# FFN norms of six images: the channel sums split into a high and a low part before TensorE adds them up

## The chip, the core and the metric

The kernel runs on one core of one Trainium2 chip. The metric is the device time of one execution in microseconds (us). A core has five engines that run their own instruction lists side by side: TensorE (PE in the profile, its weight loads PEld), VectorE (DVE), ScalarE (ACT), GpSimd (POOL) and SyncE (SP), which here only issues DMAs. They meet only at semaphores: an instruction waits until a counter has reached a value. SBUF is the on-chip memory of 128 partitions, PSUM the eight banks that TensorE writes.

## The reference, cut to what matters

Two layers run over 8 images of 384 channels and 32x32 pixels. Layer 0 is a Mamba mixer and an FFN, layer 1 a displaced 5x5 convolution and an FFN. Only the norm ahead of each FFN is touched here. Each pixel is normed over its 384 channels:

```python
def _ln_t(v, eps=1e-5):
    m = jnp.mean(v, axis=-1, keepdims=True)
    s = jnp.var(v, axis=-1, keepdims=True)
    return (v - m) / jnp.sqrt(s + eps)

def _bitlinear(x, W, b):
    Wb = _binarize_weights_groupwise(W)          # signs of W around the mean of each of 5 groups
    y = jnp.einsum('btc,oc->bto', x, Wb) + b
    return _quantize_activations_groupwise(y)    # scaled by the largest |y| of a group of images

h = _bitlinear(x, W1, b1)                        # 384 -> 1536
h = jax.nn.gelu(h, approximate=False)
out = _bitlinear(h, W2, b2)                      # 1536 -> 384

t = t + _L0_ffn_ref(_ln_t(t), ...)               # once in each layer
```

With 5 groups over 8 images a group is one image, and the last three images come out of the FFN as zeros. So each layer has five FFN images, ten in all.

## The kernel before, in words

An image lies in SBUF as `xn`, three tiles of 128 channels (partitions) by 1024 pixels. Everything of a norm is done in two halves of 512 pixels (`HALVES`, `half(h)`).

The norm of FFN image f goes through four engines:

- GpSimd adds the three tiles of `xn` into `xsum` (`sum_tiles`, L2193 and L2195), elementwise, 128x1024 each.
- TensorE multiplies `xsum` by the 128x128 matrix `mean_w`, filled with 1/384 (`norm_mean`, L1434). The product is the mean of each pixel, the same in all 128 partitions, in the PSUM banks `ph[0]` and `ph[1]`. The matmuls are in plain float32.
- VectorE subtracts it from `xn` (`norm_center`, L1872). ScalarE squares the result into `sq` (`norm_square`, L1621), GpSimd adds the three squared tiles (`sum_squares`, L2212 and L2214), TensorE multiplies the sum by `mean_w` (`norm_var`, L1446), ScalarE takes Ln and Exp of it (`norm_rstd`, L1632 and L1636), VectorE scales `xn` (`norm_scale`, L1877).
- ScalarE and VectorE split the normed image into `xh` and `xl`, a part rounded to the type float32r and the rest (`take_high`, L1647; `take_low`, L1883).

The first two images of each layer sum their squares on TensorE alone (`tiles = CT`, three matmuls a half). The other three of each layer, six images, go by GpSimd.

The order on each engine is written out by hand in its own `image(f, ...)`, in which three images overlap: while the gelu and the second product of image f run, the first product of image f+1 and the norm of image f+2 are put between them. `up(f+1, m)` (L1465) is the first product of one of 12 blocks of 128 hidden rows, 6 matmuls of float32r a half. `down(f, k)` (L1476) is the second product's step k, 12 matmuls. Each `up` writes `ph[h]`, and ScalarE reads it out (`up_bias`, L1654) before the next may write it. The norm uses the same two banks in between: `norm_mean` stands in TensorE's list between `down(f, 2)` and `down(f, 3)`, `norm_var` between `down(f, 5)` and `down(f, 6)`. Then `up(f+1, 6)` waits until VectorE has read the mean (`centered`), and `up(f+1, 9)` until ScalarE has read the variance (`ln_read`).

VectorE's list has `gelu_split(f, k)` (L1894 and L1896: clip the gelu to `gh` in float32r, and the rest to `gl`), `up_largest` (L1887, the largest of a block), and, between `gelu_split(f, 6)` and `gelu_split(f, 7)`, the two halves of `norm_center(f + 2)`.

A norm for image f+2 runs beside image f only for the first three images of a layer, f = 0, 1, 2 and 5, 6, 7 (`more2`); these six stretches are where the change acts.

## Time and profile before

| | us |
|---|---|
| median of 3 runs | 3600.06 (3598.11 to 3600.19) |
| profiled execution | 3600.21 |
| its span, first to last instruction | 3598.4 |
| mixer of layer 0 | to about 2630 |
| FFN of layer 0 | about 2630 to 3015 |
| convolution of layer 1 | about 3015 to 3208 |
| FFN of layer 1 | about 3208 to 3598 |

| engine | busy us | share |
|---|---|---|
| PE | 3329.2 | 93% |
| DVE | 3192.9 | 89% |
| ACT | 2661.7 | 74% |
| POOL | 2572.6 | 71% |

The times of the three runs and the profiled execution differ by less than the runs among themselves; the 1.8 us between 3600.21 and 3598.4 lie around the span. The shares are averages over stages that have different limits, and the mixer, which is most of the span, isn't touched. What matters is one image of an FFN, about 73 us, and in it the two places at which TensorE does the norm. A view in order of time gives start and duration of one instruction, or of several of a kind merged (x6), and in brackets how long its engine idled before it and what released it. A float32 matmul of 128x512 shows as two records.

### The profile page before, as it was taken

How to read it: one execution, taken by the hardware profiler on the slowest of the kernel's cores; microseconds unless marked ns; L12 is line 12 of the kernel's file. 1: busy time of each engine (PE TensorE's matmuls, PEld its weight loads, DVE VectorE, ACT ScalarE, POOL GpSimd, SP SyncE). 2: the span in 40 equal slices, each digit the busy share in tenths (PEclk: the TensorE clock that was granted, in tenths of full speed). 3: DMA queues.
4: the chain of work that ended last, by engine and by line, in shares of the span. 5: the costliest groups of instructions: out<-in, count | busy, mean ns of one | idle time of the engine just before them, and what ended most of it. 6: DMA issues, size and time to landing. Idle time of an engine off the chain costs nothing. (4 is left out here: it accounts for less than half of the span.)

```text
span 3598.4 us, 49955 instructions
## 1 busy us (share of the span) xinstructions
PE 3329.2 (93%) x17022; PEld 2357.5 (66%) x17022; DVE 3192.9 (89%) x3284; ACT 2661.7 (74%) x5127; POOL 2572.6 (71%) x2045
## 2 busy tenths in 40 slices
PE   7999999999998999999999999998879998889997
PEld 4666666666666666666666666666657776567776
DVE  5999999999999999999999999999867877877886
ACT  6878787788888778787877887787555555875653
POOL 4899999989999998999999899989901101551100
PEclk8999999999999999999999999999999999999998
DMA  4020220202021120202022020202210123750112
GB/s 146 2 103 29 75 81 24 86 19 99 26 83 61 43 86 19 86 19 103 28 77 86 19 86 19 103 13 82 71 62 18 55 89 116 262 185 18 71 37 89
DMA packets 83585, 249.89 MB, mean 69 GB/s; under 512 B 15212, under 2 KB 24044, under 8 KB 73092
## 3 DMA queue, kind: packets, MB, share of 16 engines
q1 hardware_dynamic: 82564, 245.65, 18.9%
q8 instruction: 137, 2.24, 0.3%
q10 hardware_dynamic: 768, 1.05, 0.1%
q14 instruction: 116, 0.95, 0.1%
HBM read 204.73 MB, written 41.95 MB: 69 GB/s over the span
## 5 line engine op out<-in xcount | busy, mean ns | idle before, releaser
L984 POOL TENSOR_TENSOR slot<-dtu,b_rep 128x512 f32<-128x512 f32 x960 | 1213.6, 1279 | 106.5 <-PE ysum L466 106.4
L994 POOL TENSOR_TENSOR slot<-slot,c_rep 128x512 f32<-128x512 f32 x864 | 1098.3, 1277 | 69.0 <-ACT carry L789 59.8
L780 ACT ACTIVATE state<-dt,aneg 128x512 f32<-128x512 f32 x960 | 657.0, 689 | 248.1 <-DVE slot L1097 175.9
L466 PE MATMUL ysum<-ident,slot 128*128 128x128 f32 x6144 | 809.2, 277 | 15.3 <-POOL slot L994 15.2
L466 PEld LDWEIGHTS ysum<-ident,slot 128*128 128x128 f32 x6144 | 713.3, 144 | 155.2 <-issue 131.4
L1089 DVE TENSOR_TENSOR_SCAN slot<-state,slot 128x512 f32<-128x512 f32 x384 | 456.2, 1204 | 52.2 <-ACT state L780 52.2
L1089 DVE TENSOR_TENSOR_SCAN slot<-state,carry,slot 128x512 f32<-128x512 f32 x384 | 478.1, 1264 | 0.0
L584 PE MATMUL state<-diag_b,dtu_t 128*128 128x128 f32 x3072 | 418.5, 280 | 55.5 <-ACT carry L789 43.8
L584 PEld LDWEIGHTS state<-diag_b,dtu_t 128*128 128x128 f32 x3072 | 381.3, 193 | 130.4 <-issue 127.8
L1097 DVE TENSOR_TENSOR slot<-state,c_rep 128x512 f32<-128x512 f32 x672 | 446.8, 667 | 0.0
L771 ACT ACTIVATE slot<-dt,aneg 128x512 f32<-128x512 f32 x576 | 404.5, 711 | 2.8 <-PE ysum L466 2.7
L1089 DVE TENSOR_TENSOR_SCAN state<-slot,carry,state 128x512 f32<-128x512 f32 x240 | 301.3, 1270 | 33.1 <-PE state L581 17.5
L1089 DVE TENSOR_TENSOR_SCAN state<-slot,state 128x512 f32<-128x512 f32 x240 | 289.5, 1215 | 33.9 <-PE state L584 21.1
L1654 ACT ACTIVATE hid<-ph_l,bias_l 128x512 f32<-128x512 f32 x240 | 164.9, 691 | 201.7 <-PE ph_l L1465 200.3
L831 ACT ACTIVATE dbu_t<-dtu_t,b_t 128x128 f32<-128x128 f32 x768 | 243.0, 389 | 0.0
L1465 PE MATMUL ph_l<-xh,w 128*128 128x512 f32 x720 | 214.7, 407 | 27.7 <-DVE xl L1883 10.9
L1465 PE MATMUL ph_l<-xl,w 128*128 128x512 f32 x720 | 207.8, 398 | 0.0
L2193 POOL TENSOR_TENSOR xsum<-xn_l 128x1024 f32<-128x1024 f32 x8 | 22.6, 2829 | 257.0 <-DMA xn_l<-between_layers 257.0
L1887 DVE TENSOR_REDUCE big_l<-hid 128x1 f32<-128x1024 f32 x120 | 144.0, 1214 | 68.2 <-ACT hid L1654 68.1
L1476 PE MATMUL acc_l<-gh,w 128*128 128x512 f32 x720 | 194.1, 406 | 7.5 <-ACT y L1681 7.5
L581 PE MATMUL state<-ident,dbu_t 128*128 128x128 f32 x768 | 124.5, 287 | 73.5 <-ACT carry L789 38.1
L1669 ACT ACTIVATE g<-hid,gain_l 128x1024 f32<-128x1024 f32 x120 | 135.4, 1149 | 68.4 <-DVE gl L1896 35.2
(288 smaller groups left out, 5943.8 us busy)
## 6 DMA issues: line engine op xcount, KB each, us to landing
c_rep<-rows_of_b_and_c SPq DMA_DIRECT2D x64, 1024.0 KB, 4.7
xres_l<-between_layers SPq DMA_DIRECT2D x18, 1536.0 KB, 9.8
xn_l<-between_layers SPq DMA_DIRECT2D x13, 1536.0 KB, 7.3
b_rep<-rows_of_b_and_c SPq DMA_DIRECT2D x16, 1024.0 KB, 4.7
between_layers<-y SPq DMA_DIRECT2D x10, 1536.0 KB, 6.3
xn<-in_x SPq DMA_DIRECT2D x16, 768.0 KB, 4.5
b_rep<-rows_of_b_and_c SPq DMA_DIRECT2D x16, 768.0 KB, 6.1
xres<-in_x SPq DMA_DIRECT2D x16, 768.0 KB, 4.5
```

What stands on the lines that cost most here:

```text
L466: last = mm(ysum[:, cols], slot[:, (NS * k + n) % SLOTS, cols], ident[:], start=first and j == 0, stop=final, is_transpose=True, skip_grou ...
L584: last = mm(state[:, q % BANKS, cols], dtu_t[:, cols], diag_b[:, diag_n().index(n), cols], start=True, stop=True)
L771: af(slot[:, q % SLOTS], dt[:, k], ACT.Exp, scale=aneg[:, k, n:n + 1]).then_inc(exp_done, 1)
L780: af(state[:, (NS * k + n) % BANKS], dt[:, k], ACT.Exp, scale=aneg[:, k, n:n + 1]).then_inc(exp_done, 1)
L831: last = af(dbu_t[:, at % SCALED, cols], dtu_t[:, cols], ACT.Copy, scale=b_t[:, h, j, n:n + 1])
L984: tt(slot[:, q % SLOTS], dtu[:, k % 2], b_rep[:, b_row(n)], ALU.mult).then_inc(dbu_done, 1)
L994: tt(slot[:, q % SLOTS], slot[:, q % SLOTS], c_rep[:, n], ALU.mult).then_inc(pool_mult_done, 1)
L1089: v.tensor_tensor_scan(to, decay, drive, carry[:, q:q + 1] if h else 0.0, ALU.mult, ALU.add).then_inc(scan_done, 1)
L1097: v.tensor_tensor(slot[:, q % SLOTS], state[:, q % BANKS], c_rep[:, n], ALU.mult).then_inc(mult_done, 1)
L1465: last = mm(ph[h][:], w1[:, t, m * P:(m + 1) * P], src[f // FFN_B][:, t, half(h)], start=p == 0 and t == 0, stop=p == 1 and t == CT - 1)
L1476: last = mm(acc[HALVES * m + h][:], w2[:, k, m * P:(m + 1) * P], src[f // FFN_B][:, k % AHEAD, half(h)], start=k == 0 and p == 0, stop=k = ...
L1654: af(hid[:, m, half(h)], ph[h][:], ACT.Identity, bias=bias1[:, f // FFN_B, m:m + 1]).then_inc(up_read, 1)
```

## The change

For the six images whose squares GpSimd sums, both sums are split before TensorE takes them. A new tile `parts` lies on the memory of `sq`. ScalarE copies the sum into `parts[:, h, 1]` rounded to float32r (the high part, `sum_high` and `square_high`, two copies of 128x512 each), GpSimd subtracts it from the sum into `parts[:, h, 2]` (the low part, `sum_rest` and `square_rest`, 128x1024), and TensorE multiplies both parts by a matrix of ones in float32r, adding them up in the bank. The factor 1/384 goes into VectorE's subtraction (now a scalar_tensor_tensor with -1/384) and into the scale of ScalarE's Ln. One copy at the start of layer 0's FFN makes the matrix `ones_r`.

```diff
+        parts = put("sum_parts", [P, HALVES, CT, T], "sq", 0, F32R)
+        ones_r = ctx.enter_context(nc.sbuf_tensor("ones_r", [P, P], F32R))
+        high_done, low_done = sem("high_done"), sem("low_done")
             def norm_mean(f):
+                if f % FFN_B >= 2:
+                    pe.wait_ge(low_done, 2 * sq_index(f) - 1)
+                    for h in range(HALVES):
+                        pe.wait_ge(up_read, HALVES * (MT * (f - 1) + MEAN_BEFORE - 1) + h + 1)
+                        mm(ph[h][:], ones_r[:], parts[:, h, 1], start=True, stop=False)
+                        mm(ph[h][:], ones_r[:], parts[:, h, 2], start=False, stop=True).then_inc(mean_full, 1)
+                    return
                 pe.wait_ge(x_summed, 2 * ln_index(f))
...
             def norm_var(f):
-                tiles = CT if f % FFN_B < 2 else 1
-                if tiles == 1:
-                    pe.wait_ge(sq_summed, 2 * sq_index(f))
+                if f % FFN_B >= 2:
+                    pe.wait_ge(low_done, 2 * sq_index(f))
+                    for h in range(HALVES):
+                        pe.wait_ge(up_read, HALVES * (MT * (f - 1) + VAR_BEFORE - 1) + h + 1)
+                        mm(ph[h][:], ones_r[:], parts[:, h, 1], start=True, stop=False)
+                        mm(ph[h][:], ones_r[:], parts[:, h, 2], start=False, stop=True).then_inc(var_full, 1)
+                    return
...
+            def sum_high(f):
+                act.wait_ge(x_summed, 2 * ln_index(f))
+                act.wait_ge(var_full, HALVES * ln_index(f))
+                for h in range(HALVES):
+                    last = af(parts[:, h, 1], xsum[f // FFN_B][:, half(h)], ACT.Copy)
+                last.then_inc(high_done, 1)
+
+            def square_high(f):
+                act.wait_ge(sq_summed, 2 * sq_index(f))
+                for h in range(HALVES):
+                    last = af(parts[:, h, 1], sq[:, h, 0], ACT.Copy)
+                last.then_inc(high_done, 1)
...
                     up_tile(f + 1, 4)
+                    if more2:
+                        sum_high(f + 2)
                     gelu(f, 5)
...
                     up_tile(f + 1, 8)
+                    if more2:
+                        square_high(f + 2)
                     gelu(f, 9)
...
                 if m == 1:
                     sign1(0, 2)
+                    act.wait_ge(consts, 1)
+                    af(ones_r[:], ones[:], ACT.Copy).then_inc(high_done, 1)
...
-                v.tensor_tensor(a, a, ph[h][:].unsqueeze(1).broadcast_to([P, CT, T]), ALU.subtract).then_inc(centered, 1)
+                mean = ph[h][:].unsqueeze(1).broadcast_to([P, CT, T])
+                if f % FFN_B >= 2:
+                    v.scalar_tensor_tensor(a, mean, -1.0 / DM, a, ALU.mult, ALU.add).then_inc(centered, 1)
...
+            def sum_rest(f):
+                pool.wait_ge(high_done, 2 * sq_index(f))
+                by_half = "p (h s) -> p h s"
+                tt(parts[:, :, 2], xsum[f // FFN_B][:].rearrange(by_half, h=HALVES), parts[:, :, 1], ALU.subtract).then_inc(low_done, 1)
+
+            def square_rest(f):
+                pool.wait_ge(high_done, 2 * sq_index(f) + 1)
+                tt(parts[:, :, 2], sq[:, :, 0], parts[:, :, 1], ALU.subtract).then_inc(low_done, 1)
...
                 sum_tiles(f)
+                sum_rest(f)
                 sum_squares(f)
+                square_rest(f)
```

GpSimd's list of one norm in layer 1's FFN, before (`xsum_...` is the tile sum, `sq` the squares; the waits are the names of the semaphores):

```order
L2193 TENSOR_TENSOR xsum_35537<-xn_l 128x1024 [waits mean_full_lead,x_loaded_l]
L2195 TENSOR_TENSOR xsum_35537<-xsum_35537,xn_l 128x1024 [waits x_summed_l]
L2212 TENSOR_TENSOR sq<-sq 128x2x512 [waits squared_lead]
L2214 TENSOR_TENSOR sq<-sq 128x2x512 [waits sq_summed_l]
L2193 TENSOR_TENSOR xsum_35537<-xn_l 128x1024 [waits mean_full_lead,x_loaded_l]
```

and of the change:

```order
L2230 TENSOR_TENSOR xsum_35538<-xn_l 128x1024 [waits mean_full_lead,x_loaded_l]
L2232 TENSOR_TENSOR xsum_35538<-xsum_35538,xn_l 128x1024 [waits x_summed_l]
L2256 TENSOR_TENSOR sum_parts<-xsum_35538,sum_parts 128x2x512 [waits high_done_l]
L2249 TENSOR_TENSOR sq<-sq 128x2x512 [waits squared_lead]
L2251 TENSOR_TENSOR sq<-sq 128x2x512 [waits sq_summed_l]
L2260 TENSOR_TENSOR sum_parts<-sq,sum_parts 128x2x512 [waits high_done_l]
```

Two instructions of 128x1024 are new, one behind the tile sum and one behind the sum of squares; both wait for ScalarE.

ScalarE's list from `gelu(f, 8)` to the Ln of the variance, before (`hid` is written by `up_bias`, `g` by `gelu`):

```order
L1669 ACTIVATE g<-hid,gain_l 128x1024 [waits g_lo_l]
L1654 ACTIVATE hid<-ph_l,bias_l 128x512 [waits up_max_l,gelu_done_l,up_full_l]
L1654 ACTIVATE hid<-ph_l,bias_l 128x512 [waits up_full_l]
L1669 ACTIVATE g<-hid,gain_l 128x1024 [waits g_lo_l] x2
L1625 ACT_TABLE_LOAD
L1632 ACTIVATE rstd_l<-ph_l,eps_t_l 128x512 [waits normed_lead,var_full_lead] x2
```

and of the change:

```order
L1696 ACTIVATE g<-hid,gain_l 128x1024 [waits g_lo_l]
L1681 ACTIVATE hid<-ph_l,bias_l 128x512 [waits up_max_l,gelu_done_l,up_full_l]
L1681 ACTIVATE hid<-ph_l,bias_l 128x512 [waits up_full_l]
L1662 ACTIVATE sum_parts<-sq 128x512 [waits sq_summed_l]
L1662 ACTIVATE sum_parts<-sq 128x512
L1696 ACTIVATE g<-hid,gain_l 128x1024 [waits g_lo_l] x2
L1638 ACT_TABLE_LOAD
L1645 ACTIVATE rstd_l<-ph_l,eps_t_l 128x512 [waits normed_lead,var_full_lead] x2
```

The two copies stand behind the read-out of `up(f+1, 8)` and ahead of gelus 9 and 10. `sum_high` stands in the same way behind the read-out of `up(f+1, 4)` and ahead of gelu 5.

TensorE's list around `norm_var`, before (`gh` and `gl` are the two parts of the gelu, each row of `acc_l` half of a `down`):

```order
L1476 MATMUL acc_l<-gl_35539,w_52 128x512 [waits g_lo_l]
L1476 MATMUL acc_l<-gl_35539,w_52 128x512 x5
L1446 MATMUL ph_l<-sq,mean_w_l 128x512 [waits up_read_l,sq_summed_l]
L1446 MATMUL ph_l<-sq,mean_w_l 128x512 [waits up_read_l]
L1476 MATMUL acc_l<-gh_35541,w_52 128x512 [waits g_hi_l]
L1476 MATMUL acc_l<-gh_35541,w_52 128x512 x5
```

and of the change:

```order
L1489 MATMUL acc_l<-gl_35540,w_52 128x512 [waits g_lo_l]
L1489 MATMUL acc_l<-gl_35540,w_52 128x512 x5
L1451 MATMUL ph_l<-sum_parts,ones_r 128x512 [waits up_read_l,low_done_l]
L1452 MATMUL ph_l<-sum_parts,ones_r 128x512
L1451 MATMUL ph_l<-sum_parts,ones_r 128x512 [waits up_read_l]
L1452 MATMUL ph_l<-sum_parts,ones_r 128x512
L1489 MATMUL acc_l<-gh_35542,w_52 128x512 [waits g_hi_l]
L1489 MATMUL acc_l<-gh_35542,w_52 128x512 x5
```

The two float32 matmuls have become four of float32r, two to a half, and the first waits for `low_done`, GpSimd's new instruction, in place of `sq_summed`.

## Rows read from the trace of the kernel before

**Rows 1.** Window of one image of layer 0's FFN: busy of PE, PEld, DVE, ACT, POOL; PEclk.
```profile
2762.00:2835.00 73.00, 72.06 (x303) 55.57 (x303) 62.74 (x61) 42.86 (x52) 10.37 (x4) 1.00 0.18 66
```

**Rows 2.** The chain that ended last, second image: start us, us, what.
```profile
2790.30 0.61 DVE gh L1894
...
2803.39 2.72 PE ph_l L1465 x12
...
2808.83 1.72 PE ph_l L1446 x4
```

**Rows 3.** Timeline of PE, second image: start us, us, engine line, [idle before].
```profile
2788.87 1.88 PE L1434 MATMUL ph_l<-xsum,mean_w_l 128*128 128x512 f32 x4
...
2791.98 1.53 PE L1476 MATMUL acc_l<-gl,w 128*128 128x512 f32 x6
2793.97 0.93 PE L1465 MATMUL ph_l<-xh,w 128*128 128x512 f32 x3 [0.46 <-DVE xn_l L1872]
...
2808.67 1.88 PE L1446 MATMUL ph_l<-sq,mean_w_l 128*128 128x512 f32 x4
```

**Rows 4.** Timeline of ACT, second image.
```profile
2781.49 1.14 ACT L1669 ACTIVATE g<-hid,gain_l 128x1024 f32<-128x1024 f32 x1
...
2795.52 1.49 ACT L1621 ACTIVATE sq<-xn_l 128x1536 f32<-128x1536 f32 x1 [0.17 <-DVE xn_l L1872]
...
2806.73 2.18 ACT L1669 ACTIVATE g<-hid,gain_l 128x1024 f32<-128x1024 f32 x2
...
2811.38 1.15 ACT L1636 ACTIVATE rstd_l<-rstd_l 128x512 f32<-128x512 f32 x2
```

**Rows 5.** Timeline of POOL, second image.
```profile
2768.09 2.40 POOL L2193 TENSOR_TENSOR xsum<-xn_l 128x1024 f32<-128x1024 f32 x1 [38.64 <-DMA xn_l<-between_layers]
2770.57 2.73 POOL L2195 TENSOR_TENSOR xsum<-xsum,xn_l 128x1024 f32<-128x1024 f32 x1
2797.09 2.51 POOL L2212 TENSOR_TENSOR sq<-sq 128x1024 f32<-128x1024 f32 x1 [23.79 <-ACT sq L1621]
2799.68 2.73 POOL L2214 TENSOR_TENSOR sq<-sq 128x1024 f32<-128x1024 f32 x1
```

**Rows 6.** Timeline of DVE, second image.
```profile
2768.45 2.59 DVE L1894 TENSOR_SCALAR gh<-g 128x1024 fp32r<-128x1024 f32 x1 [3.15 <-ACT g L1669]
2771.08 3.31 DVE L1896 SCALAR_TENSOR_TENSOR gl<-g,gh 128x1024 fp32r<-128x1024 f32 x1
...
2784.24 0.69 DVE L1894 TENSOR_SCALAR gh<-g 128x1024 fp32r<-128x1024 f32 x1
```

**Rows 7.** The chain where a GpSimd sum releases TensorE, convolution stage.
```profile
3030.18 2.35 POOL rstd_l L2208
...
3032.66 2.05 PE ph_l L1545 x2
```

**Rows 8.** The second image of layer 1's FFN: ACT's gelu 5, DVE's split 4.
```profile
3348.21 1.14 ACT L1669 ACTIVATE g<-hid,gain_l 128x1024 f32<-128x1024 f32 x1
...
3351.32 0.69 DVE L1894 TENSOR_SCALAR gh<-g 128x1024 fp32r<-128x1024 f32 x1
```

**Rows 9.** The first image of layer 0's FFN: PE, DVE.
```profile
2717.31 1.88 PE L1434 MATMUL ph_l<-xsum,mean_w_l 128*128 128x512 f32 x4
...
2717.58 0.69 DVE L1894 TENSOR_SCALAR gh<-g 128x1024 fp32r<-128x1024 f32 x1 [0.86 <-ACT g L1669]
...
2725.02 0.96 PE L1465 MATMUL ph_l<-xh,w 128*128 128x512 f32 x3 [0.31 <-ACT hid L1654]
```

**Rows 10.** The lines of two DVE operations, all of the span: duration ns min/median/max.
```profile
L1872 DVE TENSOR_TENSOR xn_l<-xn_l,ph_l x16: 1743/1746/1749, 2657.0 to 3433.4; 128x1536 f32<-128x1536 f32 x16
L1932 DVE SCALAR_TENSOR_TENSOR y<-y,xres_l x30: 1215/1218/1226, 2806.5 to 3594.1; 128x1024 f32<-128x1024 f32 x30
```

**Rows 11.** PE at a wait ahead of the change's stretches.
```profile
2649.35 0.93 PE L1465 MATMUL ph_l<-xh,w 128*128 128x512 f32 x3 [2.91 <-ACT hid L1654]
2650.12 0.85 PE L1465 MATMUL ph_l<-xl,w 128*128 128x512 f32 x3
```

More of the change, by code:

```diff
@@ L1436, in norm_var @@
             def norm_var(f):
-                tiles = CT if f % FFN_B < 2 else 1
-                if tiles == 1:
-                    pe.wait_ge(sq_summed, 2 * sq_index(f))
+                if f % FFN_B >= 2:
[5 more added lines that the diff above has]
+                    return
                 for h in range(HALVES):
-                    if tiles == CT:
-                        pe.wait_ge(squared, HALVES * ln_index(f) + h + 1)
+                    pe.wait_ge(squared, HALVES * ln_index(f) + h + 1)
                     if f != 0:
                         pe.wait_ge(up_read, HALVES * (MT * (f - 1) + VAR_BEFORE - 1) + h + 1)
-                    for t in range(tiles):
-                        last = mm(ph[h][:], mean_w[:], sq[:, h, t], start=t == 0, stop=t == tiles - 1)
+                    for t in range(CT):
+                        last = mm(ph[h][:], mean_w[:], sq[:, h, t], start=t == 0, stop=t == CT - 1)
                     last.then_inc(var_full, 1)
@@ L1631, in norm_rstd @@
                         act.wait_ge(normed, HALVES * n)
-                    af(rstd[:, half(h)], ph[h][:], ACT.Ln, bias=eps_t[:, 0:1]).then_inc(ln_read, 1)
+                    af(rstd[:, half(h)], ph[h][:], ACT.Ln, bias=eps_t[:, 0:1],
+                       scale=1.0 / DM if f % FFN_B >= 2 else 1.0).then_inc(ln_read, 1)
                 for h in range(HALVES):
@@ L1871, in norm_center @@
                 a = xn[:, :, half(h)]
-                v.tensor_tensor(a, a, ph[h][:].unsqueeze(1).broadcast_to([P, CT, T]), ALU.subtract).then_inc(centered, 1)
+                mean = ph[h][:].unsqueeze(1).broadcast_to([P, CT, T])
+                if f % FFN_B >= 2:
+                    v.scalar_tensor_tensor(a, mean, -1.0 / DM, a, ALU.mult, ALU.add).then_inc(centered, 1)
+                else:
+                    v.tensor_tensor(a, a, mean, ALU.subtract).then_inc(centered, 1)
             def norm_scale(f, h):
@@ L2244, in _ @@
                 sum_tiles(f)
+                sum_rest(f)
                 sum_squares(f)
+                square_rest(f)
 def program(nc, x, in_wT, conv_w, conv_b, xp_wT, dt_wT, dt_b, A_log, D, out_wT, W1T_0, b1_0, W2T_0, b2_0,
```

## The prediction

> **What bounds the kernel now.** I read the page first: PE 93% busy and DVE 89% over a span of which the mixer is most. That says little about the norms, so next came the windows of one image of an FFN. In 73 us PE is busy for 72.06 at full clock, DVE for 62.74, ACT for 42.86 and GpSimd for 10.37 [rows 1]. Matmuls overlap in these records, so 72.06 isn't 72.06 us of work, but PE is near its limit, and ACT and GpSimd have much room on average. The chain of waits shows which of them ends last at which place. From about 2797 to 2835 it runs through PE without a break, with the variance's matmuls in it, 1.72 us [rows 2]. Ahead of that it runs through VectorE, with the clipping of gelu 6 among its pieces, up to the two centerings [rows 2]. So the two places of the change differ: the mean is made where VectorE ends last, the variance where PE does.
>
> The timelines give the margins. The mean's matmuls start at 2788.87 and are long done when VectorE, coming from clipping gelu 6 (2790.30 in [rows 2]), gets to the centering. PE's up 6 then waits 0.46 us for VectorE, not for the mean [rows 3]. GpSimd works 10 us per image, in two bursts, and idles 24 to 39 us before them [rows 5].
>
> **TensorE's own work.** Twelve matmuls of float32r take 2.72 us, 0.227 each, at the place in question [rows 2]. The float32 pair takes 1.72. Four of float32r would take 0.91, so each of the twelve steps (two norms' steps in six images) sheds 0.81 us, 9.7 us together. The page FP8 and Floating Point Precision of the Trainium skill (TensorE Precision Notes) says that true fp32 goes through the array in four passes. By that rule one float32 matmul is worth four of the others and the step should halve, and the trace agrees: 1.72 for two is 0.86 each, 3.8 times 0.227.
>
> **The variance, six images.** Before, `norm_var` starts at 2808.67 with its sum ready since 2802.41, when GpSimd's second addition ended [rows 3, 5]. Now it waits for two more steps that can't start at 2802.41, because `square_high` stands in ACT's list behind the read-out of up 8:
> - ACT gets there at 2806.73, where gelu 9 started [rows 4], 1.94 us ahead of PE.
> - Two copies of 128x512. Two Exp of that size, SBUF to SBUF, take 1.15 [rows 4]. That gives 2807.88. From below I know nothing cheaper; from above it is twice the single read-out's 0.69, 1.38.
> - ACT to GpSimd: the square ended at 2795.52 + 1.49 = 2797.01, and GpSimd started at 2797.09 [rows 4, 5]: 0.08.
> - GpSimd's subtraction of 128x1024. The rows run from 2.35 [rows 7] to 2.73 [rows 5]. None writes float32r there, so this is a bound from neighbours. I take the 2.40 of the first addition: 2810.36.
> - GpSimd to PE: 3030.18 + 2.35 = 3032.53, PE at 3032.66 [rows 7]: 0.13. That gives 2810.49.
>
> PE stands still for 1.82 us where it stood for nothing. A restart costs 0.1 (the first three matmuls behind a wait take 2650.12 - 2649.35 = 0.77 [rows 11], against 0.68), and 0.81 comes back: 1.11 per image. The same offset of 1.94 between ACT and PE is there in all six images, since ACT is led by PE's up 8. Six times 1.11 is 6.7 us. What is queued behind the waiting matmul on PE is down 6, up 9 and all the rest of the image, and nothing later in it waits for anything but PE. Behind the ACT copies are gelus 9 and 10, the table load and the Ln. They move by 1.15 and the Ln then starts at about 2811.4, when PE has the variance; up 9, which waits for the Ln, comes only 2.7 us behind. No cost there. Clipping gelu 9 on VectorE is late by about 1.2, which VectorE's idle time ahead of the next largest takes up, PE being 1.1 later as well.
>
> **The mean, four images.** `sum_high` starts at 2781.49, where gelu 5 started [rows 4], its input ready since 2773.30. With 1.15, 0.08 and 2.40 the low part is there at 2785.12, and PE asks at 2788.87: no wait. But GpSimd is not alone. At 2768.45 VectorE started a clipping that takes 0.69 elsewhere and took 2.59, ending 0.55 behind the end of GpSimd's addition (2770.49). The next one started at 2771.08 and took 3.31, ending 1.1 behind the end of the second addition [rows 5, 6]. So GpSimd's pass stops these operations of VectorE for as long as it lasts. The new subtraction runs from 2782.72 to 2785.12. VectorE's split 4 wants to start at 2784.24, and will end at 2785.12 + 0.55 = 2785.67 and not at 2784.93 [rows 6]: 0.74 late. From there to the centering VectorE has no idle time, so up 6 starts 0.74 later too, and the 0.81 that PE sheds in `norm_mean` only lengthens its wait for VectorE. The largest-of-a-block ahead of split 4 isn't touched, as others of its kind beside GpSimd aren't.
>
> The cost depends on the distance from gelu 5 to split 4: 3.49 less the distance. It is 2.75 here and 3.11 in the second image of layer 1 [rows 8], and 2.82 and 2.69 in the two others of that pattern, the third image of each layer. The four give 0.74, 0.38, 0.67 and 0.80, 2.6 us.
>
> The page SBUF — State Buffer of the Trainium skill (Who interferes with whom) states this as an exclusive lock of a port pair that VectorE shares with GpSimd: whoever starts first keeps it for the whole instruction, and a reduction never takes part. By that rule the sum is as above, by a mere sharing of bandwidth the clipping and the subtraction would each lose a part of their 0.9 us overlap, about 0.3 an image and 1.2 in place of 2.6. The trace agrees with the lock.
>
> **The mean, first image of each layer.** There is no result of an image before to handle, and VectorE has slack: clipping gelu 6 starts at 2717.58, just when PE ends down 2 at 2717.31 and frees its buffer [rows 9] (the row names ACT, which had long finished gelu 6). GpSimd's pass delays split 5 by about 1.2 us, which ends before that. PE, ahead by 0.81, meets the centering and then ACT's read-out, as it does now at 2725.02 [rows 9]. Nothing lost, nothing gained, twice.
>
> **The rest.** Centering as scalar_tensor_tensor: 128x1024 from SBUF takes 1218 ns, the subtraction of 128x1536 takes 1746 [rows 10], both near 1.04 ns an element and 0.15 fixed. I take no difference; up to 0.1 each, in twelve, if PSUM with an immediate is dearer, 0.8 us for the eight on the chain. The scale in Ln costs nothing by itself. `ones_r` is one small copy on ACT, early in layer 0's FFN, where ACT is ahead of PE: I take 0, at most the 0.69 of one read-out. The tile is laid over `sq`, and no transfer or queue of SP changes.
>
> **Sum.** 6.7 + 2.6 = 9.3 us, on the profiled execution of 3600.2 (span 3598.4 and 1.8 around it), which is 0.15 above the median: 3609.5 us. By the bounds, copies of 1.38 and a pass of 2.73 add 0.56 at each of ten places, 5.6; a pass of 2.35 takes 0.5 away. With the mean free, 2.6 go. The forecast's own range is 3606.5 to 3615.
>
> **Rivals.**
> - *Only the variance costs* (VectorE makes up the mean's delay): 3606.9. For it: the DVE delay is under 1 us and VectorE idles 10.3 of 73 us [rows 1]. Against it: none of that idle time lies between split 4 and the centering.
> - *TensorE bounds and the parts are ready*: the place is `norm_var`, the price the 0.81 shed there in each of six images, and 3600.2 - 4.9 = 3595.3 comes out. It decides if the low part is there by 2808.67, that is if copies and subtraction together take under 1.7 us. Against it: one GpSimd pass alone takes 2.35. Only if PE's matmul and ACT's list ran otherwise than written could it hold.
> - *The low part is dearer*: GpSimd writes the rounded type or reads two operands of two kinds at, say, the 3.3 us that a hindered pass takes. 0.9 more at ten places: 3618.5. Nothing in the trace shows that form on GpSimd; VectorE writes float32r at no extra cost.
> - *The clock*: PE's new pauses of 1.8 us could make its clock fall from 2.4 to 1.2 GHz, as it isn't anywhere in this window (granted 1.00 in [rows 1]). If the next twelve matmuls ran at half speed each time, that is 2.72 us more [rows 2], six times, 16.3 and 3626 in all. Against it: a pause of 2.91 us at 2649.35 is followed by matmuls at full speed [rows 11].
>
> **How the numbers follow.** 0.60 for the forecast, 0.14 for the variance alone, 0.08 for TensorE's gain, 0.10 for the dearer part, 0.03 for the clock, 0.05 for what I don't see. A measurement of this kernel tells 0.2% from no change, 7.2 us. The forecast stands 2.1 us beyond that and its low edge inside, so I give a ninth of it to no change, and all of the second case: 0.21 same. Faster: 0.08. Slower: 0.71. The range, 3601 to 3618, leaves out the gain and the clock and half of the dearer part.
>
> **What would show it.** In the profile after: the matmuls of `norm_var` with about 1.8 us of idle PE before them, released by GpSimd's subtraction, in all six images; split 4 on VectorE at 1.0 to 1.4 us in four images instead of 0.69; up 6 waiting 1.9 us or more for the centering; no wait of PE before `norm_mean`; GpSimd's new lines at 2.4 us. If PE waits under 1 us at the variance, the sum is wrong in its main term; if split 4 keeps its 0.69, the mean's is.

## The result

The changed kernel takes 3607.02 us (median of 16 runs, 3604.97 to 3612.94), the kernel before 3599.72 us on the same chip (16 runs, 3596.83 to 3602.23). The ratio is 1.0023, 95% interval [1.0016, 1.0031]. Times 3600 that is 8.3 us slower, 5.8 to 11.2 (the two medians are 7.3 apart). The forecast was 9.3 us and 3609.5 us. Of the 15 runs of the kernel before that stand beside `mean_only_busy` below, one took 8145.35 us; the ratio leaves it out, and without it their median is 3599.51.

The profiled execution took 3606.13 us, with a span of 3604.3 against 3598.4 before. That difference, 5.9, is less than the cost of the change, because the rest of the program is not equally long in two single executions. A ruler without that noise is needed. TensorE transposes the row of largest values once per image, always at the same place in its list, so the time from one of these matmuls to the next is the length of an image. The kernel before:

```profile
2754.22 0.38 PE L1483 MATMUL ph_l<-ident_l,top_l 128*1 128x128 f32 x2
...
2826.84 0.38 PE L1483 MATMUL ph_l<-ident_l,top_l 128*1 128x128 f32 x2
```

and the kernel after:

```profile
2753.24 0.38 PE L1496 MATMUL ph_l<-ident_l,top_l 128*1 128x128 f32 x2
...
2827.60 0.38 PE L1496 MATMUL ph_l<-ident_l,top_l 128*1 128x128 f32 x2
```

2826.84 - 2754.22 = 72.62 us before and 74.36 after. The six lengths that hold a norm with GpSimd's sums (images 0 to 2 of layer 0's FFN, then of layer 1's), in us:

| | 0.0 | 0.1 | 0.2 | 1.0 | 1.1 | 1.2 | sum | less before |
|---|---|---|---|---|---|---|---|---|
| before | 67.81 | 72.62 | 72.65 | 67.13 | 72.96 | 72.56 | 425.73 | |
| after | 68.94 | 74.36 | 74.35 | 68.46 | 74.39 | 74.37 | 434.87 | +9.14 |
| after, a second execution | 68.92 | 74.30 | 74.32 | 68.29 | 74.37 | 74.36 | 434.56 | +8.83 |

The fourth length of each layer, which has no such norm in it, is 67.36 to 67.39 before and after. What is left of the span outside the six is 3172.7 before, 3169.4 and 3172.3 in the two executions after, and between 3165.7 and 3173.9 in other kernels below. So a span alone can be off by several us. The six lengths of the changed kernel repeat within some tenths (+9.14, +8.83 and, in a kernel below that differs from it by superfluous matmuls only, +9.16).

Two things besides the split norms move a length. The first is GpSimd's tile sum (L2193, L2195). It starts when a DMA has brought the image, and it holds up the splits of VectorE that it falls on, as in [rows 5, 6]. In the second image of layer 0 it starts 13.87 us behind the image's mark (2768.09 in [rows 5] less 2754.22) and the centering 37.86 behind it; in the second image of layer 1 (mark at 3320.95) they start 14.84 and 38.21 behind it. The centerings, and that later tile sum:

```profile
2792.08 3.41 DVE L1872 TENSOR_TENSOR xn_l<-xn_l,ph_l 128x1536 f32<-128x1536 f32 x2
...
3359.16 3.41 DVE L1872 TENSOR_TENSOR xn_l<-xn_l,ph_l 128x1536 f32<-128x1536 f32 x2
```

```profile
3335.79 2.39 POOL L2193 TENSOR_TENSOR xsum<-xn_l 128x1024 f32<-128x1024 f32 x1 [39.59 <-DMA xn_l<-between_layers]
```

This is why 1.1 is 72.96 and not 72.6 before. From the start of the centering to the next mark the kernel before takes 34.75 us in 0.1, 0.2, 1.1 and 1.2, within 0.01, so this part of a length is the better ruler for the variance.

The second is ahead of the split norms, at the start of each layer's first image. Behind pauses of 4.53 and 2.10 us the first matmuls run at a granted clock of 0.50, in four groups of three and a part of the fifth:

```profile
2690.06 1.65 PE L1465 MATMUL ph_l<-xh,w 128*128 128x512 f32 x3 [2.10 <-DVE xl L1883]
...
2695.34 0.98 PE L1465 MATMUL ph_l<-xh,w 128*128 128x512 f32 x3
```

The last of these groups takes 0.98 here and 1.13 in the kernel after. So the mark and `norm_mean` are 30.90 and 30.23 us apart in 0.0 and 1.0 before, and 31.06 and 30.56 after. These 0.49 us (0.31 in the second execution) are in the +9.14 but not in the norms; without them it is 8.65 (8.52). The twelve executions of changed kernels below and here have 31.01 to 31.06 and 30.37 to 30.58. With one profiled execution of the kernel before, it stays open whether its shorter stretch was chance.

**The profile after, around the variance.** TensorE's timeline in the second image, in the columns of [rows 3], which it answers to:

```profile
2807.07 1.52 PE L1489 MATMUL acc_l<-gl,w 128*128 128x512 f32 x6
2810.13 0.50 PE L1451 MATMUL ph_l<-sum_parts,ones_r 128*128 128x512 f32 x1 [1.55 <-POOL sum_parts L2260]
2810.47 0.40 PE L1452 MATMUL ph_l<-sum_parts,ones_r 128*128 128x512 f32 x1
...
2810.94 0.39 PE L1452 MATMUL ph_l<-sum_parts,ones_r 128*128 128x512 f32 x1
2811.17 1.55 PE L1489 MATMUL acc_l<-gh,w 128*128 128x512 f32 x6
```

Before, the float32 pair stood at 2808.67 with no idle time ahead of it, between these two:

```profile
2807.30 1.53 PE L1476 MATMUL acc_l<-gl,w 128*128 128x512 f32 x6
...
2811.78 1.53 PE L1476 MATMUL acc_l<-gl,w 128*128 128x512 f32 x6
```

Now four short matmuls follow a wait on GpSimd's new line. From one to the next they are 0.23 us apart; the first restarts a bit slower (0.34). What that wait consists of is in the lists of ScalarE and GpSimd at the same place; ScalarE, in the columns of [rows 4]:

```profile
2805.91 0.69 ACT L1681 ACTIVATE hid<-ph_l,bias_l 128x512 f32<-128x512 f32 x1 [0.67 <-PE ph_l L1478]
2806.49 1.14 ACT L1662 ACTIVATE sum_parts<-sq 128x512 fp32r<-128x512 f32 x2
2807.53 2.18 ACT L1696 ACTIVATE g<-hid,gain_l 128x1024 f32<-128x1024 f32 x2
```

and GpSimd, to be held against [rows 5]:

```profile
2781.73 2.41 POOL L2256 TENSOR_TENSOR sum_parts<-xsum,sum_parts 128x1024 fp32r<-128x1024 f32 x1 [9.46 <-ACT sum_parts L1656]
2796.86 2.51 POOL L2249 TENSOR_TENSOR sq<-sq 128x1024 f32<-128x1024 f32 x1 [12.72 <-ACT sq L1634]
2799.45 2.74 POOL L2251 TENSOR_TENSOR sq<-sq 128x1024 f32<-128x1024 f32 x1
2807.71 2.37 POOL L2260 TENSOR_TENSOR sum_parts<-sq,sum_parts 128x1024 fp32r<-128x1024 f32 x1 [5.52 <-ACT sum_parts L1662]
```

The sum of squares is complete at 2802.19. Then nothing happens to it for 4.3 us, until ScalarE's list reaches the copies at 2806.49. The copies and the hand-over take 1.22, GpSimd 2.37, the hand-over to TensorE 0.05. The chain of waits (the view of [rows 2]), which before ran through TensorE alone here, now goes through this work, and the 4.3 us are a part of its "issue":

```profile
2799.45 2.74 POOL sq L2251
2802.19 5.49 issue
...
2807.71 2.38 POOL sum_parts L2260
...
2810.13 0.50 PE ph_l L1451
```

**Around the mean.** VectorE's timeline beside the subtraction at 2781.73, in the columns of [rows 6]:

```profile
2783.21 1.48 DVE L1931 TENSOR_SCALAR gh<-g 128x1024 fp32r<-128x1024 f32 x1
...
2787.00 0.68 DVE L1931 TENSOR_SCALAR gh<-g 128x1024 fp32r<-128x1024 f32 x1
...
3353.67 1.12 DVE L1931 TENSOR_SCALAR gh<-g 128x1024 fp32r<-128x1024 f32 x1
```

and TensorE's, where `norm_mean` finds its parts ready and the up tile behind it waits for the centering:

```profile
2787.89 0.39 PE L1438 MATMUL ph_l<-sum_parts,ones_r 128*128 128x512 f32 x1
...
2793.74 0.93 PE L1478 MATMUL ph_l<-xh,w 128*128 128x512 f32 x3 [2.04 <-DVE xn_l L1907]
```

Split 4 takes 1.48 in place of 0.69 and ends at 2784.69, 0.55 behind the end of GpSimd's pass (2784.14). In the second image of layer 1 (3353.67), where it starts later against the pass, it takes 1.12. TensorE's wait is 2.04 where it was 0.46 in [rows 3]: VectorE is later by 0.79 and TensorE is earlier by the 0.8 that it no longer computes. Over the whole span, the waits ahead of `norm_var`, the passes and the centering (the view of [rows 10]):

```profile
L1451 PE MATMUL ph_l<-sum_parts,ones_r x12: 394/448/502, 2735.8 to 3455.2; 128*128 128x512 f32 x12
...
  POOL sum_parts L2260: 21.1, 12
```

```profile
L2260 POOL TENSOR_TENSOR sum_parts<-sq,sum_parts x6: 2365/2370/2377, 2733.4 to 3452.2; 128x1024 fp32r<-128x1024 f32 x6
```

```profile
L1907 DVE SCALAR_TENSOR_TENSOR xn_l<-ph_l,xn_l x12: 1747/1749/1751, 2717.5 to 3438.0; 128x1536 f32<-128x1536 f32 x12
```

The idle time in the first view counts the weight load (11.8 us) and the matmul (9.3 us), two for each of the six waits. The centering costs what it did, 1749 ns against 1746.

### The profile page after: what moved, and what is told of

It reads as the page before. It is cut to its first block and busy times, and to the rows that moved or that the text cites. A ratio compares the mean times of both kernels' runs of the same rounds, so it can differ in the third digit from the quotient of the medians.

```text
span 3604.3 us, 49998 instructions
## 1 busy us (share of the span) xinstructions
PE 3310.8 (92%) x17022; PEld 2348.1 (65%) x17022; DVE 3203.6 (89%) x3284; ACT 2674.3 (74%) x5152; POOL 2602.3 (72%) x2057
## 5 line engine op out<-in xcount | busy, mean ns | idle before, releaser
L581 PE MATMUL state<-ident,dbu_t 128*128 128x128 f32 x768 | 123.3, 285 | 74.2 <-ACT carry L789 38.5
L1478 PEld LDWEIGHTS ph_l<-xh,w 128*128 128x128 f32 x720 | 135.8, 195 | 82.2 <-issue 35.9
```

What stands on the lines that cost most here:

```text
L1478: last = mm(ph[h][:], w1[:, t, m * P:(m + 1) * P], src[f // FFN_B][:, t, half(h)], start=p == 0 and t == 0, stop=p == 1 and t == CT - 1)
```

## The experiments

All are edits of the changed kernel, timed in turn with the kernel before, except two second executions. "Six lengths" is the sum of the table above less the one of before. Each run has one profiled execution, so `mean_only` and the changed kernel have two. Where a sentence says how far something is behind an image's mark, the mark is that recurring matmul. The runs were made on three chips, each beside its own runs of the kernel before.

### One half at a time: var_only and mean_only

`var_only` keeps the split of the variance and takes the mean back to what it was; `mean_only` is the reverse. The core of the edit for `var_only`:

```diff
             def norm_mean(f):
-                if f % FFN_B >= 2:
-                    pe.wait_ge(low_done, 2 * sq_index(f) - 1)
...
-                    return
...
                     up_tile(f + 1, 4)
-                    if more2:
-                        sum_high(f + 2)
                     gelu(f, 5)
...
                 sum_tiles(f)
-                sum_rest(f)
                 sum_squares(f)
```

> Only the variance is split; the mean is made as before. My theory: TensorE waits 1.6 to 1.8 us for GpSimd's low part in all six images and gets 0.8 back: +1.0 an image, +6.0 us, about 3606. Split 4 on VectorE is back at 0.69. Rival (the two parts share one cost, so that either alone costs nearly all of it): 3608.

Measured: 3607.37 us against 3602.17, ratio 1.0016 [1.0007, 1.0025], six lengths +6.35. From the centering to the next mark it takes 35.76 us in all four images that have an image before them, 1.01 more than before. In the first image of a layer it is 0.96 and 1.00 from the start of down 2's gl matmuls to the next mark. The six make 6.0 us; what is left of the 6.35 comes from the two things named above, the tile sum and the slow stretch. The wait is there again, at the same size:

```profile
2812.52 0.50 PE L1444 MATMUL ph_l<-sum_parts,ones_r 128*128 128x512 f32 x1 [1.55 <-POOL sum_parts L2251]
```

> Only the mean of the six images is split; the variance is made as before, with float32 matmuls on the sum of squares. My theory: GpSimd's low-part pass stops VectorE's split 4 for 0.4 to 0.8 us in the four images behind the first of a layer, nothing in the other two, and the 0.81 us that TensorE sheds is lost in its wait for the centering: +2.7 us, about 3602.5. In the trace split 4 takes 1.1 to 1.5 us in four images and up 6 waits about 2.0 us. Rival (VectorE makes the delay up, only the variance costs): 3600, up 6 starts as far behind the image's first gelu as before.

Measured: 3605.17 us against 3602.17, ratio 1.0008 [0.9999, 1.0017], six lengths +5.84. The mean alone costs twice what was expected, and the halves add up to 12.2 where the whole is 9.1. TensorE's timeline shows where the surplus is:

```profile
2793.42 1.52 PE L1477 MATMUL ph_l<-xh,w 128*128 128x512 f32 x3 [2.04 <-DVE xn_l L1904]
2794.73 1.48 PE L1477 MATMUL ph_l<-xl,w 128*128 128x512 f32 x3
2796.01 1.29 PE L1477 MATMUL ph_l<-xh,w 128*128 128x512 f32 x3
2797.14 0.84 PE L1477 MATMUL ph_l<-xl,w 128*128 128x512 f32 x3
```

After the same 2.04 us pause as in the changed kernel, the next three rows, of three matmuls each, take 1.52, 1.48 and 1.29 and not 0.93, 0.84 and 0.94, for some 3.7 us. The window view gives a granted clock (the column behind the busy times) of 0.94 for the 30 us around it, where TensorE ran at 1.00 in [rows 1]. For the slow rows alone, 2793.40 to 2797.10, it gives 0.54, near the lower of its two levels, 1.2 GHz in place of 2.4:

```profile
2782.00:2812.00 30.00, 27.96 (x113) 21.99 (x112) 28.04 (x29) 17.12 (x21) 6.73 (x3) 0.94 0.01 3
```

Such a stretch is there in all four images with that pause. In two it begins at once. In the two others the first three matmuls behind the pause are at full speed (0.93 and 0.94), the next three a little slower (1.06 and 1.08), and the ones after that, 1.7 us behind the end of the pause, take 1.62.

### The mean's work done, but not used: mean_side

ScalarE's copies and GpSimd's pass are all there, but TensorE takes the mean from the float32 sum as before. The added wait of ScalarE's squares keeps them from writing over the low part, which lies on the memory of `sq`; the part is there 7.7 us before the centering starts.

```diff
             def norm_mean(f):
-                if f % FFN_B >= 2:
-                    pe.wait_ge(low_done, 2 * sq_index(f) - 1)
...
-                    return
...
                 act.wait_ge(centered, HALVES * n + h + 1)
+                if f % FFN_B >= 2:
+                    act.wait_ge(low_done, sq_index(f))
```

> The mean's two copies on ScalarE and GpSimd's pass are made as in the changed kernel and then not used: TensorE takes its mean from the tile sum with float32 matmuls, VectorE centers as before, the variance is as before. My theory (the mean's cost is GpSimd's pass beside VectorE, whatever TensorE does): the same +2.7 us as with the mean alone, about 3602.5, split 4 at 1.1 to 1.5 us. Rival (the cost comes from what TensorE or the centering reads): 3600, no more than 0.5 off.

Measured: 3602.55 us against 3602.17, ratio 1.0002 [0.9993, 1.0010], six lengths +2.94. Split 4 takes 1.37 us, TensorE's pause is 1.20, and its clock does not fall (three matmuls in 0.93):

```profile
2795.87 0.93 PE L1470 MATMUL ph_l<-xh,w 128*128 128x512 f32 x3 [1.20 <-DVE xn_l L1901]
```

So the mean's cost (+2.94, and +2.97 below, with 0.2 to 0.4 of it ahead of the norms) comes by the work beside TensorE alone, whatever TensorE multiplies. ScalarE's copies are in this kernel too; that it is GpSimd's pass is read from split 4, which follows VectorE's instruction before it without a wait and is itself longer.

### The pause filled: mean_only_busy, and mean_only again

`mean_only_busy` is `mean_only` with the four matmuls of the mean standing twice, so that TensorE pauses for about 1 us less ahead of the same centering. `mean_only_2` is `mean_only`, one more execution.

```diff
                         mm(ph[h][:], ones_r[:], parts[:, h, 1], start=True, stop=False)
+                        mm(ph[h][:], ones_r[:], parts[:, h, 2], start=False, stop=True)
+                        mm(ph[h][:], ones_r[:], parts[:, h, 1], start=True, stop=False)
                         mm(ph[h][:], ones_r[:], parts[:, h, 2], start=False, stop=True).then_inc(mean_full, 1)
```

> The mean alone is split and its sum over tiles stays on POOL, as in mean_only, but the four matmuls of the mean stand twice in PE's order, so that the pause of 2.04 us ahead of up's matmuls becomes about 1.1 us while the end of the mean is the same. Theory (in mean_only the pause let the clock fall, and the half-speed matmuls behind it cost about 0.65 us in each of four images beyond the 2.9 us of the wait itself): no matmul of up runs longer than 1 us there, the six stretches come back from +5.8 to about +3, as in mean_side, ratio 1.0003 to 1.0006. Rival (the clock falls for another reason, and the pause is not what matters): 1.3 to 1.5 us matmuls of up remain, the six stretches stay near +5.8, ratio near 1.001.

> A second profiled execution of the same kernel as mean_only. If the fall of the clock behind the 2.04 us pause belongs to this kernel's order of work, up's matmuls behind the pause take 1.3 to 1.5 us again in all four images and the six stretches are +5 to +6 us. If it was the luck of one execution, they take 0.84 us and the stretches are about +3 us.

Measured for `mean_only_busy`: 3600.67 us against 3599.80 (3599.51 without the long run), ratio 1.0001 [0.9992, 1.0010], six lengths +2.97 (67.91, 73.36, 73.36, 67.38, 73.35, 73.34). TensorE does more work than in `mean_only` and the images are shorter:

```profile
2791.97 0.93 PE L1479 MATMUL ph_l<-xh,w 128*128 128x512 f32 x3 [1.10 <-DVE xn_l L1906]
```

Measured for `mean_only_2`: six lengths +4.32, and both predictions of its text in one execution. In layer 0 the clock fell behind both pauses (lengths 73.97 and 74.10):

```profile
2791.38 1.53 PE L1477 MATMUL ph_l<-xh,w 128*128 128x512 f32 x3 [2.04 <-DVE xn_l L1904]
...
3358.28 0.93 PE L1477 MATMUL ph_l<-xh,w 128*128 128x512 f32 x3 [2.04 <-DVE xn_l L1904]
...
3361.94 0.97 PE L1477 MATMUL ph_l<-xh,w 128*128 128x512 f32 x3 [0.39 <-ACT hid L1680]
```

In layer 1, with the same pause, it did not, and the lengths are 73.38 and 73.37, those of `mean_side`. The last row shows why a fall costs less than the matmuls lose: at full clock up 7 waits 0.39 for ScalarE, a wait that the slow matmuls use up. Against the lengths of `mean_only_busy` one fall costs 0.59 to 0.76 us of an image, 0.68 in the mean of six. At this place it happened behind pauses of 2.04 us and not behind those of 1.1 to 1.2, and not every time: 6 of 8. By their intervals the times of `mean_only` and `mean_only_busy` are not told apart; the six lengths and the rows tell them apart. Most of why the halves did not add up is thereby explained: without falls they are 2.97 and 6.35, 9.3 together, against 9.1 of the whole.

### Is it in the changed kernel's times? after_busy and after_2

The same doubling in the changed kernel, and one more execution of it as it stands.

> The changed kernel with the mean's four matmuls done twice, so that TensorE's pause ahead of up 6 is 1.1 instead of 2.0 us. In the kernel with the mean alone a pause of 2.04 us was followed by matmuls at half speed (1.52 us for three instead of 0.84) in all four images, in the kernel with the copies beside, where the pause was 1.20, by none. My theory: the pause makes the clock fall in some executions of the changed kernel, those at 3609 to 3613 us with a granted clock of 0.972 to 0.974; with the shorter pause these go and all executions lie at 3605 to 3607, ratio 1.0018. Rival (clock and pause have nothing to do with each other): the same two groups as in the changed kernel, ratio 1.0023.

> A second profiled execution of the changed kernel. Theory (the waits set the cost): the six stretches are +9 us again, within 0.5, with the two waits of 2.0 and 1.5 us. If the clock falls behind the 2.04 us pause in some executions of this kernel and not in others, here it may fall: then up's matmuls behind it take 1.3 to 1.5 us and the stretches are about +11.5 us, which would account for part of the spread of the changed kernel's times.

Measured for `after_busy`: 3609.61 us against 3599.48 (7 runs, 3606.72 to 3611.69), ratio 1.0026 [1.0015, 1.0036], six lengths +9.16. Nothing is won by filling the pause, and the times don't come together at 3605 to 3607 us as they should have if falls of the clock made the spread. Measured for `after_2`: six lengths +8.83, and full speed behind all four pauses, the first of which is:

```profile
2796.65 0.93 PE L1478 MATMUL ph_l<-xh,w 128*128 128x512 f32 x3 [2.02 <-DVE xn_l L1907]
```

So in the changed kernel the pause of 2.0 us ahead of up 6 was not followed by a fall in any of eight images. Its cost in the profiled executions is the waits alone. Why the same pause lowers the clock in `mean_only` and not here stays open, and so does the spread of the changed kernel's runs.

### The copies ahead of the read-out: mean_early, var_only_early, both_early

The variance waits because ScalarE's copies stand behind a read-out that itself waits for TensorE. Moving them ahead of it starts them as soon as gelu 8 is done. The edit for the variance (the one for the mean is the same at tile 4):

```diff
                     gelu(f, 8)
-                    up_tile(f + 1, 8)
                     if more2:
                         square_high(f + 2)
+                    up_tile(f + 1, 8)
                     gelu(f, 9)
```

`mean_early` moves the mean's copies only, in the full change; `var_only_early` moves the variance's in `var_only`; `both_early` moves both in the full change.

> The changed kernel with sum_high one step earlier on ScalarE, ahead of the read-out of up 4, so that GpSimd's pass falls beside VectorE's reductions (from 2.2 us behind the start of gelu 4's successor slot, about 7 us ahead of split 4). My theory: split 4 back at 0.69 in all images, the mean costs nothing, what is left is the variance's +6.0: about 3606. Rival (any GpSimd pass slows VectorE by its share wherever it falls): the reductions grow from 1.21 us each and the time stays at that of the changed kernel, 3608.

Measured: 3608.30 us against 3602.17, ratio 1.0015 [1.0006, 1.0024], six lengths +7.11, 2.0 less than the changed kernel's. Split 4 is back to 0.68 us in all four images, and TensorE's pause at 1.23 in the second image. Left is the variance, as in `var_only`, and the tile sum. In 1.1 the pause is still 1.95 us, and the length 74.30: there the tile sum starts 16.4 us behind the mark (3326.69) and the centering 38.53 behind it, where 0.1 has 13.81 and 37.79. This one image holds 0.71 of the 0.76 us by which the kernel is above `var_only`:

```profile
3343.09 2.40 POOL L2230 TENSOR_TENSOR xsum<-xn_l 128x1024 f32<-128x1024 f32 x1 [33.93 <-DMA xn_l<-between_layers]
```

With the mean's pass at its late place the tile sum no longer matters: in all 28 images of the seven executions that have it (the changed kernel, `after_2`, `after_busy`, the two of `mean_only`, `mean_only_busy`, `mean_side`), the centering starts 38.56 to 38.65 us behind the mark.

> Only the variance is split, and square_high stands one step earlier on ScalarE, right behind gelu 8 and ahead of the read-out of up 8, where the sum of squares is just ready. My theory (TensorE's wait is set by where ScalarE makes the high part): the low part is there 2.5 us before TensorE asks, no wait, and the 0.81 us shed in the variance counts in each of six images, less 0.1 to 0.2 that VectorE loses behind GpSimd's pass, which now falls on split 8: -4 us against before, ratio 0.9989. Rival (what TensorE sheds is lost elsewhere, as with the mean): ratio 1.0000.

Measured: 3593.61 us against 3599.48, ratio 0.9983 [0.9974, 0.9991], six lengths -4.20. It beats both kernels, by 0.17% the one before. ScalarE and GpSimd:

```profile
2801.00 1.15 ACT L1655 ACTIVATE sum_parts<-sq 128x512 fp32r<-128x512 f32 x2
```

```profile
2802.23 2.39 POOL L2251 TENSOR_TENSOR sum_parts<-sq,sum_parts 128x1024 fp32r<-128x1024 f32 x1 [1.26 <-ACT sum_parts L1655]
```

The low part is there at 2804.62, and TensorE comes for it at 2807.22, without a wait:

```profile
2805.85 1.53 PE L1482 MATMUL acc_l<-gl,w 128*128 128x512 f32 x6
2807.22 0.39 PE L1444 MATMUL ph_l<-sum_parts,ones_r 128*128 128x512 f32 x1
...
2808.14 1.53 PE L1482 MATMUL acc_l<-gh,w 128*128 128x512 f32 x6
```

GpSimd's pass stalls VectorE here too, and for longer than at the mean, but nobody is waiting for VectorE at this place, so it costs nothing: from the centering to the next mark this kernel takes 33.93 us, 0.82 less than before, all that TensorE sheds.

```profile
2802.57 2.60 DVE L1922 TENSOR_SCALAR gh<-g 128x1024 fp32r<-128x1024 f32 x1
```

> The changed kernel with both high parts made one step earlier on ScalarE, sum_high ahead of the read-out of up 4 and square_high ahead of that of up 8. My theory: the mean costs nothing and brings nothing, the variance brings 0.7 us an image: -4 us against before, ratio 0.9989, the same as with the variance alone. Rival (the longer wait of TensorE ahead of up 6, 1.3 instead of 0.5 us, lets its clock fall): 2 to 4 us more than that.

Measured: 3594.67 us against 3599.48, ratio 0.9987 [0.9978, 0.9996], six lengths -5.16. By the lengths it is a us ahead of `var_only_early`, by the times no difference is seen. From the centering on, the two are equal (33.93 and 33.94 us). Of the 0.96 us, 0.83 are in 0.2 and 1.1, in which the tile sum of `var_only_early` fell late and its centering started 38.18 and 38.34 us behind the mark, not 37.8. So with the stall gone, the mean's split is worth next to nothing: what TensorE sheds in `norm_mean` goes into its wait for VectorE. Behind those waits, 1.1 to 1.3 us, TensorE is at full speed in all four images.

### No low part at all: high_only

This is `var_only` with the variance made of the high part alone: it leaves the low part out of the sum of squares. The core of it, against the changed kernel:

```diff
-                    pe.wait_ge(low_done, 2 * sq_index(f))
+                    pe.wait_ge(high_done, sq_index(f) + 1)
...
-                        mm(ph[h][:], ones_r[:], parts[:, h, 1], start=True, stop=False)
-                        mm(ph[h][:], ones_r[:], parts[:, h, 2], start=False, stop=True).then_inc(var_full, 1)
+                        mm(ph[h][:], ones_r[:], parts[:, h, 1], start=True, stop=True).then_inc(var_full, 1)
```

> Only the variance's high part is multiplied: the low part is left out, so the variance is that of sums rounded to float32r (this leaves part of the computation out). TensorE waits for ScalarE's copies alone and does two matmuls instead of two float32 ones. My theory: copies end 0.8 us before TensorE asks, no wait, 1.72 - 0.45 = 1.27 us gained in each of six images, -7.6 us, ratio 0.9979. Rival (the wait is ScalarE's and not GpSimd's pass): TensorE still waits about 1.7 us, ratio 1.001.

Measured: 3592.85 us against 3599.48, ratio 0.9985 [0.9976, 0.9994], six lengths -5.84, 0.97 an image and not the 1.27 expected. TensorE waits for nothing at `norm_var`, with the copies still behind the read-out:

```profile
2806.81 0.62 PE L1444 MATMUL ph_l<-sum_parts,ones_r 128*128 128x512 f32 x2
2807.27 1.55 PE L1481 MATMUL acc_l<-gh,w 128*128 128x512 f32 x6
2808.66 1.53 PE L1481 MATMUL acc_l<-gl,w 128*128 128x512 f32 x6
2810.24 0.93 PE L1470 MATMUL ph_l<-xh,w 128*128 128x512 f32 x3
```

What is late next is ScalarE's Ln at 2809.41, 1.04 us later in its list by the copies. Up 9, which waits for it, starts about 0.2 us behind the end of the matmuls ahead of it. Between `var_only` (+6.35) and this kernel lie 12.2 us, 2.0 an image: that is the price of the low part, GpSimd's pass on TensorE's path and the two matmuls that take it (0.46).

## Why the prediction was right, step by step

- **TensorE's own work** shrank as worked out: four matmuls 0.23 us apart in place of two of 0.86.
- **The variance**, 1.11 an image and 6.7 in all. Measured between the gl matmuls on either side of `norm_var`: 4.48 us before and 5.48 now (2807.07 to 2812.55), 1.00. The terms were: copies and hand-over 1.23 (1.22 measured), pass 2.40 (2.37), hand-over to TensorE 0.13 (0.05), less the 1.94 by which ScalarE is ahead (1.94 again), so TensorE stands still for 1.70 and not 1.82. The difference of 0.11 is nearly all in the hand-over to TensorE (0.08) and the pass (0.03). Six are 6.0 us, as in `var_only`.
- **The mean, four images**, 0.74, 0.67, 0.38 and 0.80. `mean_only_busy` less before, image by image, is 73.36 - 72.62 = 0.74, 0.71, 0.39 and 0.78. The step rested on a rule read from [rows 5, 6] (VectorE's clipping ends 0.55 behind GpSimd's pass) and on the distance from gelu 5 to split 4, and it held also where the distance is larger. The 0.38 for 1.1 was good for this execution of the kernel before, whose centering there was late by the tile sum; with the centering at 37.8 us behind the mark the same image would have cost about 0.8. The SBUF — State Buffer page of the Trainium skill (Who interferes with whom) calls this a lock that one of the two engines keeps for a whole instruction; the trace agrees, at 1.48 and 2.60 us for the clipping of 0.69.
- **The mean, first image of each layer**, 0. The lengths of the same kernel say 0.10 and 0.25, but that is the slow stretch at the start of the layer, ahead of the norm: from the mark to `norm_mean` it takes 31.02 and 30.48 us and not 30.90 and 30.23. From the start of down 2's gl matmuls to the next mark it is 38.26 in both, and 38.28 and 38.27 before. So it is 0, and with the four above 2.6 of the 2.97 are the mean's.
- **The rest.** The centering costs 3 ns more, twelve times. ScalarE's copies and the Ln cost nothing while TensorE waits for GpSimd; they would cost 0.2 us an image if it didn't, as `high_only` showed.
- **Sum.** 9.3 forecast, 9.14 and 8.83 in the six lengths, 8.3 [5.8, 11.2] by the times. Both mechanisms were the forecast ones. That the sum comes within 0.2 of the 9.14 is in part luck: the variance was put 0.7 us too high, and 0.5 us came at the starts of the layers, ahead of the norms, where the forecast had nothing.

Of the rivals, "only the variance costs" is refuted by `mean_side` and `mean_only_busy`, both +2.9 with no variance in them; by the times alone, 0.4 and about 1 us of difference in median with intervals that hold no change, it could not have been. "The low part is dearer" is refuted by the pass at 2.37 to 2.41. "TensorE's gain" named the right point from which it decides: where copies and pass are early enough, in `var_only_early`, the kernel gains 4.2 us against the 4.9 it named (0.82 an image from the centering on). "The clock" was argued away by a pause of 2.91 us without a fall [rows 11]. That was right for the changed kernel, and wrong as a reason, as `mean_only` shows: a fall behind a shorter pause does occur. The trace of before had a fall too, at 2690.06, behind 4.53 and 2.10 us, which the prediction did not weigh. The rival put the price too high as well, 2.72 an image against 0.6 to 0.8, because the fall is over after some nine matmuls and up 7's wait takes up a part of it.

Of the signs named for the profile, one was just missed. Split 4 was to take 1.0 to 1.4 us in four images; it takes 1.48 and 1.49 in two of them (1.12 and 1.34 in the others). In the second image that is since the distance from the copies (2780.51, where gelu 5 stood in the list before) to split 4 (2783.21) is now 2.70 and not 2.75.

## What to carry to other kernels

A chain of small steps that makes a costly matmul cheaper has to start where its input is ready, not where its engine's list happens to reach it: here 4.3 us lay unused ahead of the copies, and moving one call by one line turned +6.35 us into -4.20. When a pass is given to GpSimd, look at what VectorE does at that moment and who waits for VectorE there: the same stall cost 0.74 us at the mean of the image shown and nothing at the variance. Shortening TensorE's work ahead of a wait that another engine ends gives a longer pause and no time, and in one kernel here a lower clock behind it. And before two kernels are compared by the length of a stretch, look for what else moves it: here the arrival of a DMA set where GpSimd's tile sum fell, and with it up to 0.7 us of an image, and slow stretches of TensorE ahead of the split norms made 0.5 of the +9.14 us.

## What the runs showed of the hardware that was not expected

- The same pause of 2.04 us ahead of the same matmuls was followed by about 3.7 us at the lower clock in 6 of 8 images of `mean_only`, and in none of 8 of the changed kernel. Pauses of 1.1 to 1.3 us at this place were followed by none (`mean_only_busy`, `after_busy`, `mean_side`, `both_early`, four images each), nor were those of 1.23 to 1.95 us in `mean_early`, nor the one of 2.91 us in [rows 11]. The length of the pause alone doesn't decide it.
- More matmuls made the kernel faster: with four superfluous ones in the pause, the six lengths fell from +5.84 and +4.32 to +2.97. The times of the two kernels don't tell them apart.
- The stall of VectorE works through the old passes too. In the kernels without the mean's late pass the tile sum began 13.7 to 16.4 us behind the mark, and the later it began the later VectorE came to the centering, 37.7 to 38.5 us. With the late pass the centering stood at 38.6, wherever the tile sum fell.
- GpSimd writes the rounded type at no extra cost: 2.37 to 2.41 us for 128x1024, against 2.40 for the float32 addition of [rows 5].
